# Vision tower on one NeuronCore: second half with column-tiled squared sums, half-array routed sums, silu one slot later, and next rows turned ahead of the second down product

## The reference

```
x  = x + polymax_attention(layernorm(x)) @ W_proj        # per image, 64 tokens, causal, 16 heads
     # polymax(s) = (s*s + 1 if s > 0 else 1 - s/100 if s >= -100 else 0) / 1000
h  = layernorm(x)
u  = (h / rms(h)) @ ternary(w_up).T                      # 256 -> 1024
g  = gelu(u)
x  = x + (g / rms(g)) @ ternary(w_down).T                # rms over the 1024 columns of g
```

## Time and profile before

| | |
|---|---|
| median of 3 runs | 913.06 us (912.74 to 914.14) |
| the profiled execution, its time | 912.48 us |
| its span | 910.7 us |
| mean granted PE clock | 0.924 of full speed |
| busy: PE, PEld, DVE, ACT, POOL | 85%, 60%, 70%, 46%, 8% |
| second half, slots by their scores of tiles 2 and 3 | 530.79, 584.36, 635.57, 688.78, 741.63, 794.48, 845.41 us |

### The profile page before, as it was taken

The page is one execution under the profiler, slowest core; times in us unless marked ns, Lnnn a source line. Parts: engine busy times, 40 slices in busy tenths (PEclk is TensorE's granted clock), DMA queues, the critical chain, the costliest instruction groups (busy, mean ns, idle before and its releaser), DMA issues.

```text
span 910.7 us, 23464 instructions
## 1 busy us (share of the span) xinstructions
PE 770.1 (85%) x9831; PEld 545.5 (60%) x9831; DVE 640.8 (70%) x1443; ACT 419.9 (46%) x600; POOL 71.2 (8%) x62
## 2 busy tenths in 40 slices
PE   2769898999989898976796889898989989898966
PEld 2446665757575656655384567575866756575734
DVE  6467878777777878777598286867959676483742
ACT  3333534353535343442233563937466491745521
POOL 0000000010101010000002010000101000010000
PEclk9979999999999999995875989999999999998968
DMA  8060010101010100200000000000000000000000
GB/s 308 2 229 2 9 62 0 69 0 69 0 69 0 69 0 0 92 1 1 1 1 1 2 1 26 0 23 0 7 16 0 23 1 24 1 24 2 2 23 24
DMA packets 6779, 26.97 MB, mean 30 GB/s; under 512 B 2256, under 2 KB 3152, under 8 KB 5072
## 3 DMA queue, kind: packets, MB, share of 16 engines
q1 hardware_dynamic: 6736, 26.35, 7.8%
HBM read 22.15 MB, written 4.19 MB: 29 GB/s over the span
## 4 chain that ended last, share of the span: by engine, by line
PE 39%; issue 33%; DVE 17%; ACT 7%; POOL 2%; DMA 1%; DVEq 0%; POOLq 0%; SPq 0%; ACTq 0%
PE PS L335 8%; PE PS L695 5%; PE PS L660 3%; PE PS L637 3%; PE PS L346 2%; PE PS L325 2%; PE PS L683 2%; PE PS L673 2%; PE PS L554 2%; PE PS L631 2%; PE PS L651 2%; PE PS L307 2%; ACT w_s L955 1%; PE PS L438 1%; DVE wup_s L1468 1%
## 5 line engine op out<-in xcount | busy, mean ns | idle before, releaser
L673 PE MATMUL PS<-xT,wqkv_h 128*128 128x512 f16 x256 | 70.8, 431 | 23.9 <-ACT w_s L955 22.1
L307 PE MATMUL PS<-tokW_h,w_s 128*128 128x256 f16 x576 | 67.7, 278 | 16.3 <-DVE w_s L1311 16.3
L830 ACT ACTIVATE Pm<-Pm 128x1024 f32<-128x1024 f32 x32 | 33.9, 1058 | 83.7 <-DVE Pm L1237 83.7
L307 PEld LDWEIGHTS PS<-tokW_h,w_s 128*128 128x128 f16 x576 | 56.8, 100 | 24.1 <-issue 16.3
L1573 DVE TENSOR_TENSOR work<-w_s,work 128x512 f16<-128x512 f32 x48 | 32.5, 689 | 47.5 <-ACT work L957 47.5
L837 ACT ACTIVATE PT<-PS 128x512 f32<-128x512 f32 x64 | 37.5, 596 | 59.8 <-PE PS L428 59.8
L1030 POOL TENSOR_TENSOR rstd<-ve,mhalf 128x4 f32<-128x4 f32 x24 | 28.0, 1168 | 470.1 <-DVE ve L1146 470.1
L673 PEld LDWEIGHTS PS<-xT,wqkv_h 128*128 128x128 f16 x256 | 25.1, 107 | 64.5 <-ACT w_s L955 32.4
L325 PE MATMUL PS<-ident_s,xn 128*128 128x128 f32 x256 | 45.6, 302 | 15.5 <-DVE xn L1150 14.9
L335 PE MATMUL PS<-xT,wat_h 128*128 128x512 f16 x192 | 48.3, 414 | 7.6 <-DVE xT L1509 7.6
L695 PE MATMUL PS<-tokW_h,work 128*128 128x256 f16 x448 | 51.3, 273 | 0.5 <-DVE msq L1580 0.5
(11 more groups left out here) (243 smaller groups left out, 1643.8 us busy)
## 6 DMA issues: line engine op xcount, KB each, us to landing
work<-in_x SPq DMA_DIRECT2D x8, 1536.0 KB, 6.4
out<-H SPq DMA_DIRECT2D x8, 512.0 KB, 2.6
w_s<-in_w SPq DMA_DIRECT2D x3, 1024.0 KB, 6.9
wup_s<-in_wup SPq DMA_DIRECT2D x1, 1024.0 KB, 5.3
wdn_s<-in_wdn SPq DMA_DIRECT2D x1, 1024.0 KB, 7.3
w_s<-in_tokW SPq DMA_DIRECT2D x1, 768.0 KB, 7.5
wup_s<-in_wqkv SPq DMA_DIRECT2D x1, 768.0 KB, 8.1
wdn_s<-in_s SPq DMA_DIRECT2D x3, 256.0 KB, 6.0
```

The source lines that it names most:

```text
L307: m = pe.matmul(dst, halves_[xi][:, k, rows], w[:, wi, k, cols], start=(n == 0), stop=(n == 3 * chunks - 1))
L673: m = pe.matmul(PS[:, UP_BANKS[f % 4], :], wup_h[:, c, f * P:(f + 1) * P], part[:, c, :], start=(k == 0), stop=(k == 2 * C - 1))
```

## The change

Everything is in the second half.

1. **Gram in column tiles, half of it earlier.** Only the diagonal of g times g transposed is wanted, so for each 32 tokens a product of a 128 x 32 stationary with 64 columns (the high and the low part of the same 32 tokens) does: 16 small matmuls per f instead of 4 of 256 columns. Four of them write four 32-partition strips of bank 6. All fits in bank 6, so gram runs four groups behind the up products; groups 4 to 7 stay at the head of the next slot. Up products rotate through three banks (4, 7, 5) and wait for gelu f-3. Mean squares read 64 columns instead of 256.
2. **ACT and DVE during the up products.** Each rounding is issued behind the next gelu. The squares of tiles 0 and 1 move from ACT to DVE (v_quads).
3. **Routed sums in two half-array tiles** (even and odd k on partitions 0 to 63 and 64 to 127), folded by one matmul at the end; the second table is used in its unturned form.
4. **Silu one slot later**: silus and weighted_hots move from the end of slot g to the start of g+1 on DVE, one_hots behind them, and the sums go behind K and Q on PE. The first (empty) batch of sums goes, with POOL's two memsets.
5. **Next rows turned ahead** of the second down product (banks 4 and 3), with the low part of x and the output rows on DVE ahead of the polynomials of tiles 2 and 3; K ahead of the statistics.

```diff
-        UP_BANKS = (4, 6, 7, 5)
-        GRAM_LAG = NF
+        UP_BANKS = (4, 7, 5)
+        GRAM_LAG = 4
+        X3_BANKS = (4, 3)
...
@@ routed_sums
                 for k in range(RB):
-                    m = pe.matmul(PS[0:64, 2, 0:HID], one_hot_w[:, k, :], wz_k[:, k, :],
-                                  start=(k == 0), stop=(k == RB - 1))
+                    half = slice(64 * (k % 2), 64 * (k % 2) + 64)
+                    m = pe.matmul(PS[half, 2, 0:HID], one_hot_w[:, k, :], wz_k[:, k, :],
+                                  start=(k < 2), stop=(k >= RB - 2))
...
@@ B3_up
-                    if f >= 4:
-                        pe.wait_ge(g_ok, NF * g + f - 3)
+                    if f >= 3:
+                        pe.wait_ge(g_ok, NF * g + f - 2)
...
@@ gram
                 for t in range(TILES):
-                    m = pe.matmul(PS[:, 6 + t // 2, (t % 2) * E:(t % 2 + 1) * E], G_hi[:, f, t * P:(t + 1) * P],
-                                  G_both[:, f, :, t * P:(t + 1) * P], start=(f == 0 and t % 2 == 0),
-                                  stop=(f == NF - 1), skip_group_check=True)
+                    for i in range(4):
+                        at = t * P + 32 * i
+                        m = pe.matmul(PS[32 * i:32 * i + 32, 6, t * 64:(t + 1) * 64], G_hi[:, f, at:at + 32],
+                                      G_both[:, f, :, at:at + 32], start=(f == 0 and t == 0), stop=(f == NF - 1),
+                                      tile_position=(0, 32 * i), skip_group_check=True)
...
@@ B3_down
-                    if t % 2 == 0:
-                        pe.wait_ge(msq_ok, TILES * g + t + 2)
+                    if t == 2:
+                        pe.wait_ge(msq_ok, TILES * g + TILES)
...
@@ B3_down_last
                     if f >= NF - GRAM_LAG:
-                        pe.wait_ge(g_ok, NF * g + NF)
                         gram(g, f)
...
@@ a_B3 (ACT)
-                    act.activation(g32[f], PS[:, UP_BANKS[f % 4], :], ACT.Gelu).then_inc(g_ok, 1)
-                    act.wait_ge(g_ok, NF * g + f + 1)
-                    act.activation(G_hi[:, f, :], g32[f], ACT.Copy).then_inc(gh_out, 1)
+                    act.activation(g32[f], PS[:, UP_BANKS[f % 3], :], ACT.Gelu).then_inc(g_ok, 1)
                     if f < 2 and nxt:
-                        quads(g + 1, f)
                         lins(g + 1, f)
+                    if f > 0:
+                        g_high(g, f - 1)
+                g_high(g, NF - 1)
...
@@ (DVE)
+            def v_quads(g, t):
+                dve.wait_ge(relu_ok, TILES * g + t + 1)
+                v = relu_s[t % 2][:, :]
+                dve.tensor_tensor(v, v, v, ALU.mult).then_inc(quadv_ok, 1)
...
@@ gated_sums
-                dve.wait_ge(racc_ok, LAST - 1)
-                dve.scalar_tensor_tensor(out=gm[:, :], in0=racc[:, :], scalar=0.5, in1=tabC[:, :], op0=ALU.mult,
-                                         op1=ALU.mult).then_inc(gm_ok, 1)
+                dve.wait_ge(gT_mm, 1)
+                dve.wait_ge(tabT_ok, 2)
+                dve.scalar_tensor_tensor(out=gT[:, :], in0=PS[:, 0, 0:64], scalar=0.5, in1=AC[1][:, :], op0=ALU.mult,
+                                         op1=ALU.mult).then_inc(gT_ok, 1)
...
@@ (POOL)
-            pool.wait_ge(cnt_ok, 1)
-            for buf in (wz, tz):
-                pool.memset(buf, 0.0).then_inc(routed_zero, 1)
...
@@ (each engine)
             slot_B(0, False, True)
-            with pe.Fori(1, LAST - 2) as i:
+            slot_B(1, True, True, routed="first")
+            with pe.Fori(2, LAST - 2) as i:
                 slot_B(i, True, True, routed="batch")
```

178 lines of the change are left out of this document (95 added, 83 removed).

## The result

The changed kernel takes 876.15 us (median), the kernel before 913.45 on the same chip: a ratio of 0.960 [0.956, 0.964], 37 us less. The forecast was 889, with 879 to 903 as the range; the time lies 3 us under its low end. So the direction held and the size did not: the change is worth 35 to 37 us where the sum said 24.

The account below looks back on a forecast made before the run. Head and middle were taken as bound by PE, up products by ACT, with DVE just behind. Terms -15.4 - 3.9 - 2.8 + 1.9 - 2.1 + 1.3 - 3.4 = -24.4 from 912.48 gave 888.1, median 889 us; range 879 to 903.

Parts of the forecast that it names:

- junction: Up products, scores and gram, seven times: half the gram moved earlier, squares to DVE; 2.2 us each, 15.4 in all.
- mechanism of the stretch: From a slot's first up product to the next slot's first values: DVE last, with PE 0.9 us ahead.
- 20 ns a matmul: Column-tiled gram: price near the fp32 values product's 17 ns, the lower end; 0.32 us per group of 16.
- floor of some 25 ns: Small gram matmuls: 25 ns start to start would make the head 0.3 us longer per junction, the sum 891.
- Drains: Rival: PE empties itself around gram groups between full-array products, 0.9 x 7 = 6 us, so 895; chance 0.10.
- The middle of a steady slot: Slots 2, 3, 4, up to second values: sums 1.77 instead of 3.54, DVE's K last; 1.3 us each, 3.9.
- slot 1: With neither sums nor silu there, the middle ends 5.0 us earlier, 2.8 beyond the junction.
- Slot 0: K starts near 494.6, not 496.71, as low x no longer stands behind two polynomials: -2.1 us.
- The end: From the last up products on: up products 9.3 us, four grams at half clock 2.6; -3.4 us in all.
- Slots 5 to 7: Beyond the junction: slots 5 and 6 change by 0; slot 7, without Q and K to cover polynomials, +1.9 us.
- Ahead of slot 0: Before slot 0: two squares cost DVE 2.4 us on the row codes' path, POOL's memsets go; +1.3 us.

Follow-up runs that it names:

- second profile: The changed kernel run again without any edit, for another profile: 878.5 us, 0.962 of the kernel before; profile span 877.7.
- E4: Changed kernel with all eight gram groups in the head, none between the up products: 885.9 us, 0.971 of the kernel before.
- E5: Changed kernel with six gram groups in the head and two behind the seventh and eighth up products: 883.9 us, 0.967 of the kernel before.
- E11: Changed kernel with DVE's first polynomial ahead of low parts 0 and 1, ACT reordered, six gram groups in the head: 862.7 us, 0.943 of the kernel before.
- E2: Kernel before with only the narrow gram, 128 small matmuls in the head: 909.9 us, 0.996 of the kernel before.
- E3: Changed kernel with every gram matmul issued twice: 903.9 us, 0.991 of the kernel before.
- E7: Changed kernel with all 32 routed-sum matmuls on one tile again, partitions 0 to 63: 884.7 us, 0.968 of the kernel before.
- E10: Changed kernel with DVE's order altered in slots 5 to 7, gated sums and polynomials moved earlier: 869.9 us, 0.952 of the kernel before.
- E8: Changed kernel with the squares of tiles 0 and 1 back on ACT: 896.5 us, 0.980 of the kernel before.

## Why the prediction was low, step by step

The step that failed first is the size of the junction, "each junction gives 2.2 us, all seven 15.4": measured are 2.2 to 4.1, 21.4 in all. Between the 24.4 of the forecast and the 33.0 of the second profile lie 8.6 us: the seven stretches have 6.0 of them, slot 0 3.3, the end 1.8, the slots behind their first values 1.2, and the time ahead of slot 0 took 3.7 more than forecast. The mechanism held; three terms were too small.

**The mechanism of the stretch held: DVE is last, PE just ahead.** The waits came where the prediction put them (gram 0, gram 2 ahead of the eighth up product, the head's last group), and E4, E5 and E11 show that PE's own work there can grow or shrink without changing it. Its size was off: 2.2 forecast, 3.0 measured in slot 3, 3.1 in the mean of seven. The forecast took the stretch before as the same seven times; slot 0's was 21.32 (PE waited 1.97 for gelus twice there) and fell by 4.1. I laid DVE's row out with the mean duration of its records, 0.69 for a low part, while starts are 0.60 to 0.61 apart (725.04 to 725.64), since an operation begins before the record of the one ahead ends. The row is 10.1 us long where I had 10.6, and ACT's first rounding, behind operations that start before the record ahead ends, is out 5.3 behind the first relu instead of 5.5. The trace of before had it already: the last two low parts of slot 3 start at 691.94 and 692.55.

**Gram: 20 ns a matmul forecast, 8 to 9.5 measured** (E2, E3), under the lower bound of 17 that I drew from a row of fp32. That bound was wrong, and the earlier trace rows could have told it: a record of 128 x 256 takes 0.25 in fp32 (8 in 1.99) and 0.115 in fp16 (32 in 3.67). Half of 17 is 8.5. I used the fp32 records to raise the price and did not ask what a record of fp16 costs. It matters little: with DVE last, 0.3 to 0.7 us less of gram in the head is a shorter wait. Where PE is the bound, at the end, it counts.

**The Trainium skill's floor of some 25 ns under small matmuls** (TensorE: Matmul & The Clock Gate, "Wait — 56ns, not 53.3ns?") does not hold for these column-tiled ones: 128 in 1.03 and in 1.21 us. **Drains** are not to be seen at the rival's price: a whole group of 16 between full-array products sets the next product back by 0.23, and one of 32 by 0.34 to 0.35 (E3, 788.32 to 788.66). If 16 more matmuls cost 0.11 to 0.12, entry and exit together cost about as much. The Trainium skill's rule that a change of tiling mode drains the TensorE (TensorEngine Tiling, "Key Properties") may be behind that 0.12; no run told it apart.

**The middle of a steady slot: 1.3 forecast, 1.6 measured** (second values 18.9 behind the first instead of 20.55). Sums at half the time held (E7). The forecast had DVE's K end last; in fact PE comes 0.2 later and does not wait, again because DVE's row was laid out too long. In slot 1 it was 2.4 instead of 2.8; that row gave 6.5 because the stretch ahead of it gave 4.1.

**Slot 0: 2.1 forecast, 4.9 to 5.4 measured, and this step failed by a size that I had in a row.** K and Q started where I said (494.43 for 494.6). But they took 5.34 instead of 8.12. I took the 8.12 as a property of slot 0. In two profiles with a wait of 4.1 to 4.2 before them they took 8.12 and 8.04; in twelve profiles with a wait of 1.5 to 1.7, 5.34 each time. The windows of the kernel before show it:

```profile
492.60:494.60 2.00, 0.00 (x0) 0.00 (x0) 1.97 (x4) 0.60 (x1) 0.00 (x0) 1.00 0.00 0
...
496.71:500.00 3.29, 3.29 (x8) 1.14 (x9) 1.75 (x6) 0.00 (x0) 0.00 (x0) 0.50 0.00 0
```

The granted clock was 1.00 when the wait of 4.11 began and 0.50 when K and Q started. Who shortens such a wait gets the clock too.

**The end: 3.4 forecast, 4.7 to 5.2 measured.** I took the 9.3 us of the up products for a time at the lower clock. They were not: it was 0.50 for their first 4 us and 1.00 from 885 on. On top I put four gram groups at half clock (2.6 in all) and 0.9 for a slow start of the down products. Up products and gram groups together took 11.2 and 10.7 us instead of 11.9, since the gram groups ran at full clock (0.30 each) behind low parts that were there already. The down products started at full clock (32 matmuls in 3.67).

**Slots 5 to 7** gave what the stretch gave, and the 1.9 forecast as lost in slot 7 is there to 0.1 (1.4 of gain from a stretch worth 3.3). The waits behind it are the ones that E10 took away. In slot 6 the projection behind such a wait was slow in both profiles (3.56 and 3.46 for 1.99); in the first the scores behind it were too, and the two differ by 1.8.

**Ahead of slot 0: 1.3 forecast, 1.1 measured**, once it is taken from a mark near by. From the first V product (L617 before, L618 after) to the first values it is 28.64 and 28.65 us in the two profiles without the changed setup, and 29.70 to 29.72 in eleven of the twelve with it; in the twelfth, E8, the squares are back on ACT and it is 27.43. The rest of the +0.7 and +5.0 arose in the first half, which the change does not touch: the first values start anywhere between 484.6 and 489.5 in the twelve.

**The range** left too little room on the low side. I let it end where gram cost 17 ns and PE's waits went. Every size was rounded toward care, and I did not ask what the sum is if all of them are a fifth too small in the same direction, though they came from the same two habits: record lengths taken as distances, and slow stretches taken as fixed.

**Parts do not add.** Undone one at a time in the changed kernel, the squares cost 18.0 us, the turned rows 13.6, the gram 9.0 and the sums 6.2: 46.8, against 35 for the whole change, whose losses elsewhere are in that too. The narrow gram alone, put on the kernel before, gives 3.6. Here each part was worth more with the others in place. One reading is that the others had already made its engine the late one; of the four only the gram was tried both ways.

## What to carry to other kernels

Lay an engine's row out with the distance between starts, not with record lengths, and start a chain of waits at the first idle gap: the 1.88 us in which DVE waited for one rounding was worth 16 us over seven slots once an independent polynomial was put into it. Before removing work from an engine, look at what it will wait for next (E2: in two heads 1.7 and 1.9 of 2.4 us came back at once). And price a wait of PE with what stands behind it: where the next products run at the lower clock, short groups with waits between them cost more behind than in themselves.
